# A two-layer gated cross-attention kernel: where the first layer's drain issues its padding transfers and writes the rest of its tile list

## The reference

```python
x = x + tanh(g_xattn[0]) * xattn0(layernorm(x), ctx, ctx, mask)
x = x + tanh(g_ffn[0])   * ffn0(layernorm(x))      # 8 experts, hidden 512, one expert per token
x = x + tanh(g_xattn[1]) * xattn1(layernorm(x), ctx, ctx)
x = x + tanh(g_ffn[1])   * ffn1(layernorm(x))      # 16 experts, hidden 64, two per token, bounded capacity
```

## Time and profile before

| what | us |
|---|---|
| median of three runs (526.56, 528.28, 531.51) | 528.28 |
| the profiled execution's own time | 529.13 |
| its span, first to last instruction | 527.0 |
| TensorE / VectorE / ScalarE / GpSimd busy | 448.2 / 366.4 / 321.6 / 273.6 |
| granted TensorE clock, mean share of full | 0.968 |

### The profile page before, as it was taken

One profiled execution on the slowest core, in us unless ns is written; L12 is line 12 of the kernel. 1 busy time (PEld: TensorE's weight loads), 2 busy tenths in 40 slices (PEclk: granted clock), 3 DMA queues, 4 the chain that ended last, 5 costly groups with the idle time before them and its releaser, 6 DMA issues.

```text
span 527.0 us, 22052 instructions
## 1 busy us (share of the span) xinstructions
PE 448.2 (85%) x8481; PEld 327.5 (62%) x8481; DVE 366.4 (70%) x977; ACT 321.6 (61%) x764; POOL 273.6 (52%) x325
## 2 busy tenths in 40 slices
PE   2788899899978795999997899988997787988887
PEld 1455676667656685999973566756665565444444
DVE  5678788979778765455534779898989687453355
ACT  2455576566756773677745466776776466675554
POOL 2631634655466178888886326544425406542555
PEclk9999999999999998999999899999999898599999
DMA  7124344132111155465435011010121000000112
GB/s 202 50 55 125 95 124 123 59 112 68 44 52 33 34 137 86 78 92 73 37 35 146 3 43 34 14 33 24 27 69 34 13 4 2 2 1 11 36 48 70
DMA packets 50630, 30.69 MB, mean 58 GB/s; under 512 B 12384, under 2 KB 46944, under 8 KB 50528
## 3 DMA queue, kind: packets, MB, share of 16 engines
q1 hardware_dynamic: 37072, 18.54, 13.2%
q0 software_dynamic: 6640, 4.67, 6.9%
q10 hardware_dynamic: 6816, 6.07, 4.1%
HBM read 19.41 MB, written 9.85 MB: 56 GB/s over the span
## 4 chain that ended last, share of the span: by engine, by line
PE 44%; DVE 21%; issue 15%; POOL 9%; ACT 5%; DMA 3%; ACTq 1%; DVEq 1%; SPq 0%; POOLq 0%
DVE maxes L604 8%; POOL x_mid L1153 7%; PE T_ps L871 6%; PE S_ps L860 6%; PE A_ps L886 4%; PE m_H_ps L1440 3%; PE S_ps L854 2%; PE f_H_ps L1205 2%; PE m_T_ps L1480 2%; PE m_X_ps L1467 2%; DVE prob L612 2%; PE Q_ps L753 2%; PE Q_ps L841 2%; PE m_X_ps L1423 2%; PE f_Y_ps L1219 2%
## 5 line engine op out<-in xcount | busy, mean ns | idle before, releaser
L604 DVE TENSOR_REDUCE maxes<-S_ps 128x8 f32<-128x512 f32 x128 | 87.5, 684 | 41.0 <-PE S_ps L860 41.0
L431 POOL TENSOR_TENSOR k_blk<-kT,col_a 128x512 f32<-128x512 f32 x64 | 67.7, 1067 | 81.7 <-ACT kT L492 56.0
L534 ACT ACTIVATE probT<-T_ps 128x512 f32<-128x512 f32 x128 | 76.1, 594 | 48.2 <-PE T_ps L871 47.6
L612 DVE TENSOR_TENSOR prob<-S_ps,maxes 128x512 f32<-128x512 f32 x128 | 88.5, 692 | 4.4
L871 PE MATMUL T_ps<-col_a,prob 128*128 128x128 f32 x512 | 83.8, 288 | 8.1 <-DVE prob L612 4.7
L871 PEld LDWEIGHTS T_ps<-col_a,prob 128*128 128x128 f32 x512 | 57.0, 144 | 46.5 <-issue 33.7
L1153 POOL DMA_INDIRECT x_mid<-f_out,f_rows x39 | 60.9, 1562 | 12.4 <-issue 10.1
L860 PE MATMUL S_ps<-k_blk,qT 32*64 32x256 f32 x1024 | 46.9, 414 | 6.1 <-DVE prob L612 4.4
L1018 DVE TENSOR_TENSOR f_hid<-f_H_ps,f_b 128x512 f32<-128x512 f32 x39 | 27.0, 692 | 33.9 <-PE f_Y_ps L1219 28.5
L886 PE MATMUL A_ps<-v_blk,probT 128*32 128x18 f32 x4096 | 48.7, 188 | 0.2 <-issue 0.2
L886 PEld LDWEIGHTS A_ps<-v_blk,probT 128*32 128x32 f32 x4096 | 42.1, 111 | 9.6 <-issue 8.7
(11 more groups left out here) (202 smaller groups left out, 881.3 us busy)
## 6 DMA issues: line engine op xcount, KB each, us to landing
f_w<-in_W ACTq DMA_DIRECT2D x16, 256.0 KB
ctxT<-in_ctxT SPq DMA_DIRECT2D x12, 256.0 KB, 3.1
f_rows<-sorted_rows SPq DMA_DIRECT2D x39, 64.5 KB, 2.0
out<-m_final SPq DMA_DIRECT2D x32, 64.0 KB, 1.5
x_all<-in_x SPq DMA_DIRECT2D x6, 256.0 KB, 5.9
x_mid<-x_all SPq DMA_DIRECT2D x6, 256.0 KB
x_all<-x_mid SPq DMA_DIRECT2D x6, 256.0 KB, 4.2
ctxT<-in_ctxT SPq DMA_DIRECT2D x8, 128.0 KB, 2.5
```

What stands on the lines that cost most here:

```text
L431: nc.gpsimd.tensor_tensor(k_blk[:, t % 2, :, :, :], kT[:, g.at(R), t - g.first, :].rearrange("p (b k) -> p b k", b=2).unsqueeze(2).to_broa ...
L534: nc.scalar.activation(probT[:, t % 2, 4 * h:4 * h + 4, :], T_ps[:, :, :], ACT.Exp, scale=SCALE).then_inc(probT_ready, 1)
L604: nc.vector.tensor_reduce(maxes[:, t % 2, h, :, :], half_of(h), X, ALU.max).then_inc(max_ready, 1)
L612: nc.vector.tensor_tensor(prob[:, t % 2, heads, :].rearrange("p (r e) k -> p r e k", r=2), half_of(h), maxes[:, t % 2, h, :, :].unsqueeze( ...
```

## The change

VectorE's `list_rest` moves from 39 to 39.05, so it comes behind the VectorE steps of slot 8. SyncE issues all eight padding transfers, and ScalarE none.

```diff
@@ drain_vector
-                (take_full, once, lambda _: FULL_AT + 2), (list_rest, once, lambda _: REST_AT), (note(1), once, lambda _: REST_AT + 0.7)] + placed(tile_vector(dve))
+                (take_full, once, lambda _: FULL_AT + 2), (list_rest, once, lambda _: REST_AT + 0.05), (note(1), once, lambda _: REST_AT + 0.7)] + placed(tile_vector(dve))
@@ drain_sync
-        return [(load(sp), range(FULL_TILES), lambda t: FULL_AT + 2.5), (pad_ends(sp, range(0, E0, 2)), once, lambda _: REST_AT)]
+        return [(load(sp), range(FULL_TILES), lambda t: FULL_AT + 2.5), (pad_ends(sp, range(E0)), once, lambda _: REST_AT)]
@@ drain_scalar
-        return [(warm, once, lambda _: NT - 0.5)] + placed(sooner, 0.1) + [(pad_ends(eng, range(1, E0, 2)), once, lambda _: REST_AT)] + placed(later)
+        return [(warm, once, lambda _: NT - 0.5)] + placed(sooner, 0.1) + placed(later)
```

## The result

The changed kernel is 0.79% slower: the ratio to the kernel before is 1.0079, with a 95% interval of 1.0054 to 1.0105, from 20 runs of each. On 531.45 us, the median of the kernel before, that is 4.2 us (2.9 to 5.6). The medians of all runs, 534.05 us and 531.45 us, lie only 2.6 us apart: the ratio is taken from the runs in the chip's fast state, and the medians from all of them. The predicted difference of 3.4 us lies between these two numbers and inside the interval. The three runs from which the prediction started had a median of 528.28, 3.2 us under that of twenty. The absolute forecast of 531.7 is 2.35 us under 534.05, less than that base was low.

The account below looks back on a forecast made before the run. TensorE and GpSimd were taken as nearly tied over the stage. Tile 13 late by 1.4 us plus 2.0 us of clock gave +3.4 us: 528.28 + 3.4 = 531.7 us, range 527.3 to 534.8.

Parts of the forecast that it names:

- Tile 13 is 1.4 us late, the clock takes 2.0: Sum for TensorE from tile 13 on: late rows plus half clock put the last send 3.4 us later.
- ScalarE's copy of tile 8 and TensorE's first hole: Without pads ScalarE copies tile 8 early, up(8) starts near 203.0, and TensorE idles from 204.8 to 207.8 for the list.
- When the pads begin: VectorE's list starts at 204.97 after bias and finish, 1.8 us later; SyncE's first pad goes out at 205.86.
- Eight pads in a row: SyncE issues eight pads in steps of 1.11 us, the last at 213.6, landing 3.1 us later (2.0 to 4.8).
- Tile 13: TensorE turns it at 219.4, 1.4 us later (0.3 to 3.1), after about 6 us idle, since load(13) awaits the pads.
- The clock: TensorE falls to half clock after the hole before tile 13, costing 1.7 to 2.4 us, taken as 2.0.
- The end: The whole kernel ends 3.4 us later; slower by more than 1% was given 0.16.
- GpSimd's tie: Over the whole stage GpSimd's back-to-back sends nearly tie with TensorE; its two pauses exceed the usual by 0.23 and 0.29 us.
- The rival in which nothing is lost: Tile 13's rows are in by 218.05, GpSimd's chain sets the end: -0.5 us, 527.8; chance 0.14.
- The rival in which the clock stays up: TensorE keeps full clock at tile 13, so only +1.4 us remains, 529.7; chance 0.08.
- The one of slow landings: SyncE's eighth pad lands later than 218.2 and the clock is lost in full: +5.5 us, 533.8; chance 0.16.
- One queue or two: By the skill's rule SyncE's pads land no quicker alone; giving up ScalarE costs four issues, 4.4 us.

Follow-up runs that it names:

- after_2: The changed kernel unaltered, measured again beside the kernel before; ratio to the kernel before 1.0079 (1.0044 to 1.0114).
- after_again: The changed kernel unaltered, measured again on a chip where everything up to the drain took 20 us longer; ratio to the kernel before 1.0053 (1.0014 to 1.0092).
- fill_hole: The changed kernel with four unused identity matmuls on TensorE ahead of the turn of tile 13; ratio to the kernel before 1.0006 (0.9977 to 1.0036).
- before_fill: The kernel before with four unused identity matmuls ahead of up(8) and the first-matrix wait moved ahead; ratio to the kernel before 0.9957 (0.9915 to 0.9999).
- split_6_2: The changed kernel with the region-ends cast ahead of slot 8, six pads on SyncE, two on ScalarE; ratio to the kernel before 1.0021 (0.9987 to 1.0055).
- pads_alone_2: The kernel before with all eight pads on SyncE, list still ahead of slot 8, second run; ratio to the kernel before 1.0024 (0.9989 to 1.0058).
- sets 2 and 3: Two groups of follow-up runs, on two chips whose times are like those of the first result; ratios to the kernel before from 0.9957 to 1.0079.
- pads_alone: The kernel before with all eight pads on SyncE, list still ahead of slot 8, on a slower chip; ratio to the kernel before 0.9974 (0.9927 to 1.0020).

## Why the prediction was right or wrong, point by point

What failed is the size of both terms of the sum "Tile 13 is 1.4 us late, the clock takes 2.0", the clock's most. In the profiled execution the clock took 3.0 us and tile 13 was 2.0 us late. Beside it, the reading failed that a change within 1% is "about what a measurement of this kernel can tell from no change": with twenty runs of each kernel the interval is 0.26% to each side, and a ratio of one lies outside it.

- *ScalarE's copy of tile 8 and TensorE's first hole:* right. The copy ran at once, and `up(8)` followed the turn of tile 9 without idle time. TensorE then waited 3.56 us for the list (3.0 forecast).
- *When the pads begin:* the step "203.09 + 0.76 + 0.83 + 0.29" was too short by 0.34 us, because I let `finish(5)` wait for nothing, and the cast took 0.37 us longer than the row of before. The first pad went out 3.49 us behind the last row cast, where I had 2.77. Why the cast was slower no run shows; it took 0.15 us in after_2 and after_again.
- *Eight pads in a row:* right, at 1.10 us each (I had 1.11). The landing of the last took 2.8 us, the largest of eight, against 3.1 assumed and 3.0 to 4.8 when two queues sent at once.
- *Tile 13:* 2.0 us later than before, where I said 1.4; right in place and cause (a pad's landing ends the wait), small by the 0.7 us above. The hole before it was wrong: I had about 6 us and it is 3.84. TensorE came to tile 13 13.13 us behind the last row cast, not 10.4, since the list was turned 0.7 us later than forecast and slots 10 to 12 took 7.7 us and not 5.7; the clock was at half for 3.41 us there.
- *The clock:* the mis-sized term. I took 2.0 us with 2.4 as the upper end, from two stretches of the trace before, and gave as the reason that the new hole is longer than 4.92 us. In the profiled execution it is shorter, and the loss is larger all the same: 3.0 there, and 1.7 and 2.7 in other runs of the same kernel. So the length of a hole does not give the loss. That the loss is there, and is on the path, fill_hole shows.
- *The end:* +4.9 us in the trace, which is 2.0 + 2.9; the ratio says +4.2 (2.9 to 5.6). I forecast +3.4 and gave 0.16 to more than 1%. The direction and the mechanism hold, both terms were small by about a third of what this trace shows, and "within 1%" is where the ratio lies, although its interval reaches past it.
- *The last send* starts at 278.48, where I had 278.4. That agrees by luck: the drain began 1.42 us earlier, and from its start the last send came 1.5 us later than forecast.
- *GpSimd's tie:* right, by before_fill. It is why a version with the pads well spread (split_6_2) only gets back to the kernel before.
- *The rival in which nothing is lost* did not occur with the change; pads_alone_2 came near it. *The rival in which the clock stays up* is refuted by all traces of the changed kernel. The one of slow landings came near the size in the trace (+5.5, measured 4.9) for the wrong reason: the landings were quick.
- *One queue or two:* eight pads on one queue cost 8.03 us of issue against 3.67 on each of two, and landed no later, but sooner (2.1 us in the median, where it was 3.7 and 3.2). With the sentence of the Trainium skill ("Trainium Kernel Development and Optimization", Key Constraints) that several issuing engines only save issue time, the trace agrees in so far as two queues landed nothing sooner; that the landings differ at all the sentence does not say.

Which part is to blame stays open in the times: neither alone is clear of no change. In the traces of sets 2 and 3 and the first result the list's move costs 1.9 us, the pads' move about nothing, and both together 2.4 to 4.9. My reading, argued from the traces and not tested by itself, is this: with the pads' move alone the hole and the half clock are there too, but tile 13 comes 1.1 us sooner than before the change, which pays for the half clock. The later cast pushes all eight pads by 2.5 us; tile 13 is then late already, and the half clock comes on top.

## What to carry to other kernels

An instruction that lets another queue begin (here a cast of eight numbers) is best placed by what waits for it, not together with the list in whose function it happens to stand; the traces favour that here, the times do not prove it. Before work is moved off an engine to fill a hole, look at what the freed engine reaches next: here it came, four tiles on, to a transfer that had been hidden, and paid there in idle time and then in half clock. Where a second engine's chain is back to back beside the one that looks like the bound, a gain on the first is worth only the pauses of the second.

## What was not expected

The length of a hole says little of the half clock behind it. Ahead of tile 13 it was 2.87 us (hole of 3.14), 3.41 (3.21), 3.36 (6.07), 5.43 (5.24) and 6.04 us (3.84), and none behind 1.93 and 0.79 us of idle time. Part of a half-clock stretch can pass in the hole, where it costs nothing: of pads_alone's 6.07 us some 3.5 did (mean clock 0.71). Earlier in the drain a hole of 3.17 us left the clock full, and one of 2.42 us did not. Windows of fill_hole and of split_6_2, the hole and then what follows:

```profile
206.26:209.43 3.17, 0.00 (x0) 0.00 (x0) 2.74 (x15) 0.89 (x2) 2.67 (x2) 1.00 0.39 55
209.43:215.35 5.92, 5.92 (x53) 5.92 (x54) 2.84 (x6) 3.84 (x9) 4.70 (x5) 1.00 0.58 108
```

```profile
204.39:206.81 2.42, 0.00 (x0) 0.00 (x1) 1.75 (x6) 0.74 (x2) 2.12 (x2) 0.95 0.46 143
206.81:210.00 3.19, 3.19 (x15) 3.11 (x16) 2.20 (x12) 2.15 (x6) 2.58 (x3) 0.50 0.86 85
```

And four matmuls of no use, 3.60 us, put into the hole before tile 13 changed the ratio by 0.7%, nearly as much as the whole change had cost.
